# A four-layer conditioned sequence block: the next batch's opening is moved one stage ahead, into the scores and the attention tail

## The reference, cut to what matters

```python
# L0: layer norm with a conditioned bias
out = (x - mean) * rsqrt(var + 1e-5) * weight + bias + tanh(cond @ lin_w.T + lin_b)
x = out * weight + bias
# L1: bottleneck whose two matrices depend on cond (the "down" and "up" products)
down = relu(x @ Wd_b.T + bd);  x = x + down @ Wu_b.T + bu
# L2: RMS norm, up_w (2*1024 x 256), val * gelu(gate), quantised, ternary down_w, + x
# L3: adaptive RMS norm, attention with 16 heads of 16, then SwiGLU
x = x + (cond @ attn_alpha_w.T) * attention(ada_rmsnorm(x))
x = x + (cond @ ffn_alpha_w.T) * (swiglu(ada_rmsnorm(x)) @ out_w.T + out_b)
```

## Time and profile before

| what | value |
|---|---|
| median of three runs | 692.21 us |
| profiled execution | 697.42 us |
| its span on the core | 695.6 us |
| mean granted clock of TensorE | 0.972 of full speed |
| TensorE busy | 626.0 us, 90% |
| VectorE busy | 416.1 us, 60% |
| ScalarE busy | 393.5 us, 57% |
| GpSimd busy | 90.8 us, 13% |

### The profile page before, as it was taken

How to read it: one execution, slowest core, us unless ns; L and a number is a source line. 1 busy time by engine, 2 the same in 40 slices (tenths; PEclk the granted TensorE clock), 3 DMA queues, 4 the chain that set the end, 5 groups by cost and what they waited for, 6 DMA issues and landing times.

```text
span 695.6 us, 9460 instructions
## 1 busy us (share of the span) xinstructions
PE 626.0 (90%) x3495; PEld 420.0 (60%) x3495; DVE 416.1 (60%) x840; ACT 393.5 (57%) x755; POOL 90.8 (13%) x117
## 2 busy tenths in 40 slices
PE   3765798899989999999989999999899999999896
PEld 1421577754457878744458878644478787444585
DVE  0341697498536575788265765986365857881444
ACT  1322478336775558367873675467755583677610
POOL 1002330121000000631000002710000006310000
PEclk9976699999999999999999999999999999999999
DMA  8998640512000001431000005320000005210000
GB/s 261 373 356 286 191 143 31 114 24 50 1 1 1 1 1 44 101 77 25 1 1 1 0 8 110 82 47 2 2 1 0 1 7 109 68 34 2 0 1 31
DMA packets 34877, 45.06 MB, mean 65 GB/s; under 512 B 4752, under 2 KB 27920, under 8 KB 34704
## 3 DMA queue, kind: packets, MB, share of 16 engines
q1 hardware_dynamic: 30128, 31.32, 16.2%
q0 software_dynamic: 3488, 10.49, 5.4%
q10 hardware_dynamic: 1216, 2.66, 1.4%
HBM read 28.45 MB, written 3.15 MB: 45 GB/s over the span
## 4 chain that ended last, share of the span: by engine, by line
PE 61%; DVE 14%; ACT 10%; DMA 8%; issue 3%; SPq 2%; ACTq 1%
PE psum L1314 27%; PE psum L1566 8%; DVE mx L1143 8%; PE psum L1555 7%; PE psum L1512 7%; DMA arena<-in_hyp_w 3%; DMA early_pieces<-in_hyp_w 3%; PE psum L1458 2%; DMA kst<-split 2%; ACT arena L615 2%; PE psum L1394 2%; PE psum L1594 2%; PE psum L1403 1%; ACT arena L689 1%; ACT act L615 1%
## 5 line engine op out<-in xcount | busy, mean ns | idle before, releaser
L1143 DVE TENSOR_REDUCE mx<-psum 128x1 f32<-128x512 f32 x256 | 159.7, 683 | 32.0 <-PE psum L1512 32.0
L829 ACT ACTIVATE arena<-psum 128x512 f32<-128x512 f32 x256 | 140.5, 601 | 61.0 <-PE psum L1555 59.3
L1314 PE MATMUL psum<-act,ghw_hi 128*128 128x512 f32 (+1 forms) x288 | 88.5, 375 | 3.0 <-DVE act L955 2.5
L1512 PE MATMUL psum<-kst,qst 96*128 96x512 f32 x192 | 79.2, 437 | 2.9 <-DMA kst<-split 1.2
L1555 PE MATMUL psum<-qst,kst 98*128 98x512 f32 x192 | 77.6, 425 | 1.8 <-ACT arena L829 1.8
L1314 PE MATMUL psum<-upw_hi,kst 128*128 128x512 f32 x256 | 72.2, 404 | 0.0
L452 POOL DMA_DIRECT2D kst<-split x36 | 18.0, 505 | 411.7 <-DMA kst<-split 371.1
L1566 PE MATMUL psum<-arena,vals 128*17 128x512 f32 x512 | 67.4, 598 | 1.4 <-ACT arena L829 1.0
L1314 PEld LDWEIGHTS psum<-act,ghw_hi 128*128 128x128 f32 x288 | 51.9, 188 | 14.6 <-DVE act L955 4.7
L1512 PEld LDWEIGHTS psum<-kst,qst 96*128 96x128 f32 x192 | 36.1, 189 | 40.4 <-DVE mx L1143 30.4
L1314 PEld LDWEIGHTS psum<-upw_hi,kst 128*128 128x128 f32 x256 | 47.1, 191 | 9.6
(11 more groups left out here) (199 smaller groups left out, 1109.2 us busy)
## 6 DMA issues: line engine op xcount, KB each, us to landing
early_pieces<-in_hyp_w SPq DMA_DIRECT2D x17, 512.0 KB, 8.7
arena<-in_hyp_w SPq DMA_DIRECT2D x15, 512.0 KB, 8.5
qst<-split SPq DMA_DIRECT2D x72, 64.0 KB, 3.5
kst<-split POOLq DMA_DIRECT2D x36, 128.0 KB, 3.6
arena<-in_x SPq DMA_DIRECT2D x4, 512.0 KB, 3.5
arena<-in_up_w POOLq DMA_DIRECT2D x8, 256.0 KB, 4.0
arena<-in_gh_w POOLq DMA_DIRECT2D x8, 256.0 KB, 3.3
out_x<-arena SPq DMA_DIRECT2D x8, 256.0 KB, 2.1
```

Source lines behind the costliest of these rows:

```text
L829: s.activation(probs[:, kb % 2, i, :], bank[3 + n % RING], ACT.Exp).then_inc(a_p, 1)
L1143: v.reduce_max(mx[:, g % 2, col:col + 1], bank[u % RING], AX.X).then_inc(d_max, 1)
L1314: ins = pe.matmul(dst, lhs(a, c), rhs(z, c), start=start and n == 0, stop=stop and n == len(terms) - 1, skip_group_check=skip)
L1512: pe.matmul(bank[u % RING], qst[g % 3][0:KROWS, i, P * t:P * t + P], keys_of(g)[0:KROWS, i // 2, :], start=True, stop=True).then_inc(e_max, 1)
```

## The change

The next batch's front starts one stage earlier, and its last parts leave the feed-forward stage.

- Norm: GpSimd now takes the power -1/2 of the variance (`front_root`, two operations of 128x4) instead of ScalarE's root and VectorE's reciprocal, and VectorE's `front_norm` stands in score group 3, directly behind the statistics and the weights.
- Turn: in two parts of four transposes (`front_turn_part`), into banks 5 and 6, one in front of and one behind `turn_heads` of the last group.
- x1: ScalarE writes only the two high parts (`front_x1_high`), in the tail. VectorE makes the full value from PSUM itself (`front_x1`, into a new place `x1T`) and the low part (`front_x1_low`).
- Down product: behind the attention output, into bank 7; the Relu pair of `front_bottleneck` stands between `half_affine` and the first Silu, its low part on VectorE in front of block 0.
- Alphas: for batches 1 to 3 the product is made in two halves of 256 columns in the tail of the batch before (bank 6), around the transposes of the norm. VectorE makes `wo_alpha` from PSUM and copies the second half to a place that alternates between the two halves of the tile `alpha` (`ff_alpha`). In batch 0 it stays where it was.
- The up product and what follows it move one block forward; the three products of `keep_clock` in the tail go, except in the last batch.

```diff
-FRONT_BANK = (6, 7)
+FRONT_BANK, DOWN_BANK, ALPHA_BANK = (5, 6), 7, 6
...
+            def front_root(f):
...
+                pool.wait_ge(d_mv, f + 1)
+                pool.sem_inc(keys_free, 1)
+                pool.tensor_scalar(stat[:, RS0, :], mv[:, :, 1], 1e-5, None, ALU.add).then_inc(p_rs0, 1)
+                pool.wait_ge(p_rs0, 2 * f - 1)
+                pool.tensor_tensor(stat[:, RS0, :], stat[:, RS0, :], neg_half.to_broadcast([P, T]), ALU.pow
+                                   ).then_inc(p_rs0, 1)
...
                 if not last:
-                    deviation(b + 1)
+                    front_x1_high(b + 1, 0)
                 for h in range(2):
                     heads_turned(1, h)
+                if not last:
+                    front_x1_high(b + 1, 1)
...
+                if not last:
+                    front_bottleneck(b + 1)
                 for f in range(HT if last else NOW):
...
                     if not last:
-                        if f == 0:
-                            front_x1(b + 1)
                         if f == 1:
-                            front_bottleneck(b + 1)
-                        if f == 2:
                             front_h2(b + 1)
...
+            def front_x1(f, c):
+
+                v.wait_ge(a_x1, (f + 1) * C + c + 1)
+                step(v.tensor_scalar(x1T[:, c, :], bank[FRONT_BANK[c]], w_sq[:, c:c + 1],
+                                     prm_all[:, f, Q_B0 + c:Q_B0 + c + 1], ALU.mult, ALU.add))
...
+            def front_alphas(f):
+
+                v.wait_ge(e_alpha, f + 1)
+                v.wait_ge(p_wo_alpha, 1)
+                v.tensor_tensor(wo_alpha[:, :, :], vow[:, 1, :].rearrange("p (c d) -> p c d", c=C),
+                                bank[ALPHA_BANK][:, 0:D].unsqueeze(1).to_broadcast([P, C, D]), ALU.mult)
...
+                            condition(b + 1)
+                            front_norm(b + 1)
...
                 if not last:
-                    front_norm(b + 1)
+                    front_x1(b + 1, 0)
+                    front_x1_low(b + 1, 0)
+                    front_x1(b + 1, 1)
                 for h in range(2):
                     pair = slice(2 * h, 2 * h + 2)
                     v.wait_ge(e_wo, b * 2 + h + 1)
...
+                if not last:
+                    front_x1_low(b + 1, 1)
...
+                if not last:
+                    front_bottleneck(b + 1)
+                    front_alphas(b + 1)
...
-                        if g == 1 and k == AT_ALPHA:
+                        if g == 1 and k == AT_ALPHA and first:
                             alphas()
...
-                if not last:
-                    front_turn(b + 1)
-                keep_clock(bank[0], 6 if last else 3)
+                if last:
+                    keep_clock(bank[0], 6)
+                else:
+                    front_down(b + 1)
+                    front_alphas(b + 1, 0)
                 for h in range(2):
                     turn_half(b, h, d_xn4, e_n2T, bank[4 + h], xn4)
+                if not last:
+                    front_alphas(b + 1, 1)
...
                     if f == 0 and not last:
-                        pe.wait_ge(a_x1, (b + 1) * (2 * C) + 2 * C)
+                        pe.wait_ge(a_dn, (b + 2) * 2)
+                        pe.wait_ge(d_alpha, b + 2)
...
                     if not last:
                         if f == 1:
-                            front_down(b + 1)
-                        if f == 2:
                             front_up(b + 1)
```

More of the change, by code:

```diff
@@ L123, in build @@
         consts = sb("consts", [P, 4])
-        eps5, eps6, magic = consts[:, 0:1], consts[:, 1:2], consts[:, 2:3]
+        eps5, eps6, magic, neg_half = [consts[:, k:k + 1] for k in range(4)]
         bn = sb("bn", [P, T, 6])
@@ L152, in build, with ff_alpha @@
         kept_hh = (kept_even, kept_odd)
+        def ff_alpha(b):
+            return alpha[:, D:2 * D] if b % 2 == 0 else alpha[:, 0:D]
         hidden_raw = hypw[:, 1, :]
@@ L562, in batch @@
                 alphas(b, first)
+                if b < B - 1:
+                    front_root(b + 1)
             batch(0, first=True)
@@ L641, in front_x1, with front_x1_high @@
                 affine(f, e_l0T, lambda c: bank[banks[c]], slice(0, L), None, Q_B0, inp[0], a_x1, full)
+            def front_x1_high(f, c):
+                s.wait_ge(e_l0T, f * C + c + 1)
+                s.activation(inp[0][:, c, :], bank[FRONT_BANK[c]], ACT.Identity, scale=w_sq[:, c:c + 1],
+                             bias=prm_all[:, f, Q_B0 + c:Q_B0 + c + 1]).then_inc(a_x1, 1)
             def front_bottleneck(f, full=dn_f):
@@ L645, in front_bottleneck @@
                 for dst in (dn_s[0], full):
-                    s.activation(dst, bank[4], ACT.Relu, bias=vec[:, V_BD:V_BD + 1]).then_inc(a_dn, 1)
+                    s.activation(dst, bank[4 if f == 0 else DOWN_BANK], ACT.Relu, bias=vec[:, V_BD:V_BD + 1]).then_inc(a_dn, 1)
             def front_h2(f):
@@ L1050, in batch @@
             def batch(b, last, first=False):
-                v.tensor_copy(cond_bc[:, :], condT[:, bass.ds(b, 1)].to_broadcast([CND, P])).then_inc(d_prm, 1)
+                if first:
+                    condition(0)
                 v.wait_ge(d_rs2, b + 1)
@@ L1180, in batch @@
                             u += 1
-                        if g == 1 and k == ALPHA_OUT:
-                            if not first:
-                                v.wait_ge(p_kept_ff, b * 2)
+                        if g == 1 and k == ALPHA_OUT and first:
                             alphas()
@@ L1337, in front_turn, with front_turn_part, front_alphas @@
                 turn(f, d_xn, e_l0T, [bank[k] for k in banks], x_tok)
+            def front_turn_part(f, c):
+                pe.wait_ge(d_xn, f * T + T)
+                for t in range(T):
+                    ins = pe.transpose(bank[FRONT_BANK[c]][:, P * t:P * t + P], x_tok[:, t, P * c:P * c + P], ident[:, :])
+                ins.then_inc(e_l0T, 1)
+            def front_alphas(f, h):
+                if h == 0:
+                    pe.wait_ge(d_prm, f + 1)
+                    pe.wait_ge(a_x1, (f + 2) * C)
+                ins = pe.matmul(bank[ALPHA_BANK][:, D * h:D * h + D], cond_bc[:, :], alphaw[:, D * h:D * h + D],
+                                start=True, stop=True)
+                if h == 1:
+                    ins.then_inc(e_alpha, 1)
             def front_down(f, first=False):
@@ L1341, in front_down @@
                 pe.wait_ge(d_x1, f * C + C)
-                product(bank[4], lambda a, c: hyp_s[a][:, c * BN:(c + 1) * BN], lambda a, c: inp[a][:, c, :],
+                product(bank[4 if first else DOWN_BANK], lambda a, c: hyp_s[a][:, c * BN:(c + 1) * BN], lambda a, c: inp[a][:, c, :],
                         range(C)).then_inc(e_down, 1)
@@ L1651, in batch @@
                 weigh(NG - 1, T - 1)
+                if not last:
+                    front_turn_part(b + 1, 0)
                 for h in range(2):
                     turn_heads(NG - 1, h, range(2 * h, 2 * h + 2))
+                if not last:
+                    front_turn_part(b + 1, 1)
                 for h in range(2):
@@ L1693, in batch @@
                     ins.then_inc(e_gh, 1)
-                    if f == 4 and not last:
+                    if f == 3 and not last:
                         front_x2tok(b + 1)
```

52 lines of the change are left out of this document (34 added, 18 removed).

## The result

The changed kernel takes 698.19 us (median of 22 runs, 693.63 to 701.81) where the kernel before, on the same chip, takes 693.59 us (22 runs, 690.56 to 698.57). The ratio is 1.0059, 95% interval [1.0043, 1.0076]: slower by 0.6%. Forecast were 690.6 us and no change. A second measurement of both, further down, gives 1.0055 [1.0031, 1.0078].

A forecast was written before the change was run, and what follows sets the result against it. It took one TensorE stream, held in places by other engines, as the bound. Three steps of +2.0 + 0.15 - 1.4 give +2.25, with scores -3.9 makes -1.65 us: 692.21 to 690.6 us, range 686.5 to 695.5.

The forecast's parts named there:

- some tails: Rival: TensorE's clock falls in one or two tails, about 1.4 us a tail, 692.0 to 693.4 us; chance 0.14.
- Slower: Rival: clock falls in all three tails from the down product into feed-forward, 1.9 us or more each, 696.3 us; chance 0.07.
- Tail, +2.0: Tail: down product and alpha half before the turn start `half_affine` 2.0 us later, 0.7 of the addition included.
- First block, +0.15: First feed-forward block: TensorE waits 0.8 us for Relu, table and alphas, instead of 0.65 us for `front_x1`: +0.15 us.
- Down product gone from the stream, -1.4: Feed-forward stream on TensorE: `front_down` is missing from it, 1.4 us less a step.
- scores, -1.3: Scores of batches 1 to 3: without the alpha product and its copy, 1.3 us less a batch, -3.9 us over three.
- Norm in the scores, 0: Scores: norm and condition copy hide in VectorE's 6.96 us idle time if GpSimd's two operations take under about 5 us; cost 0.
- Turn and x1 fit into the tail's pauses: Tail: eight transposes fit TensorE's waits within 0.1 us; ScalarE's x1 fits its wait, but VectorE's addition comes 0.7 us later.
- if the granted clock is 0.5 anywhere behind the pause: Sign named beforehand that the prediction is wrong: half clock behind TensorE's pause of about 2 us before the down product.
- the tail is nearly free: Rival: engine pauses in the tail take up the moved work, delay 1.6 us, scores give 1.6; 686.1 us; chance 0.21.
- GpSimd's power is slow: Rival: power over 10 us makes the norm hold up VectorE's last heads; at 12 us, 696 us; chance 0.03.
- The table rule: Rival: a 1.38 us drain behind table loads; if only behind the Relus, hidden block 1.1 us later a step, 693.9; chance 0.03.

The follow-up runs named there:

- b_nokeep: The kernel before without its three clock-keeping products in the tails of batches 0 to 2; 693.63 us, ratio to before 1.0010.
- after_again: The changed kernel, unaltered, measured once more on the chip of the variants; 697.10 us, ratio to before 1.0055.
- fill8: The changed kernel with eight 128x512 products without use in TensorE's pause before the down product, batches 0 to 2; 692.89 us, ratio to before 0.9996.
- alpha_back: fill8 with the alpha product of batches 1 to 3 put back among the score tiles; 696.46 us, ratio to before 1.0026.
- pe_order: The changed kernel with nine filling products and, on TensorE, first-half turn, down product, second-half turn, then alphas; 687.76 and 689.00 us, ratios to before 0.9922 and 0.9936.
- no_fill: The changed kernel, pause unfilled, with first-half turn before the down product and VectorE's additions and first norm before x1 chunk 1; 693.02 us, ratio to before 0.9989.

## Why the prediction was wrong, point by point

**The step that failed** is the choice of full clock for the forecast, together with the sentence on the clock-keeping products, "they stood in front of a wait and cost nothing". Their removal is not the whole of it: in the kernel before, where the gap that they leave is 0.90 us, it costs nothing that can be measured (b_nokeep); here it leaves a pause of 1.98 us without cover. The prediction had seen the pause of 2 us, had found the same pause before the one fall in the trace, and then gave clock falls only 0.14 and 0.07. From the down product on, one fall makes a step of after 1.4 to 2.3 us longer than its undisturbed one. That is the mechanism of both clock rivals: *some tails* by the count (two of three tails in each of the two profiles), *Slower* by the place, the reach and the price (1.9). That *Slower* forecast 696.3 us, 4.1 us above its 692.21, and that the measured loss is 0.0059 x 693.59 = 4.1 us too, is partly luck: it took three falls off a gain of 1.65 us. The profile of after_again has two falls of 2.15 us, 4.3 us, less a gain of 0.1 to 0.3 us in each of the three steps, which makes its three steps 4.0 us longer than before's. The argument against it, "one case, not a rule, and the places around the pause are busy", was the wrong way round: one pause of that length was known, and it had fallen. The Trainium skill's "TensorE: Matmul & The Clock Gate", section "HAM oscillation", which says that kernels that wait between bursts come back at half clock, agrees with this in kind; the traces add that it does not happen behind every such pause.

**Term by term, at full clock** (step 1 of after, and fill8, whose steps average 148.07 against before's 148.34). Split at the first output product, the step is:

| | before | fill8 | difference | forecast |
|---|---|---|---|---|
| mark to first output product | 15.95 | 18.14 | +2.19 | +2.15 |
| from there to the next mark | 132.39 | 129.93 | -2.46 | -2.7 |
| step | 148.34 | 148.07 | -0.27 | -0.55 |

- *Tail, +2.0*: `half_affine` is 2.33 us later (9.35 against 7.02). Several terms were a little short: x1 of chunk 1 takes 0.81 us and not 0.69, the down product keeps the queue for 1.53 us (200.95 to 202.48) and not 1.40, the alpha half for 0.63 and not 0.55, the turn until `half_affine` 0.69 and not 0.6. With the alpha half gone altogether `half_affine` comes 0.79 us sooner (alpha_back).
- *First block, +0.15*: TensorE's wait before the output product is 0.51 us (from VectorE) instead of 0.8, less than before's 0.65, so this term is -0.14. VectorE's four operations ahead of the block take 2.67 us together (208.01 to 210.68), and not the 2.99 of their added lengths. That the sum of the two terms is right to 0.04 is luck: their errors have opposite signs.
- *Down product gone from the stream, -1.4, and scores, -1.3*: together -2.46; by alpha_back the scores are -1.22, which leaves -1.24 for the first, if nothing else changed in that stretch.
- *Norm in the scores, 0*: right. GpSimd's power takes 1.32 us and VectorE waits 0.81 us for it at 183.39, in its idle time.
- *Turn and x1 fit into the tail's pauses*: right; the attention output starts 2.50 us behind the mark in both kernels, and VectorE waited 0.17 us for ScalarE before x1 of chunk 1.

So the mechanism was right at each place it was worked out, and the sum at full clock is -0.8 us over three steps where -1.65 was forecast. Against the falls that error is small. Of the signs named beforehand, "if the granted clock is 0.5 anywhere behind the pause" came, and so did a step that grows.

**Of the other rivals**: *the tail is nearly free* did not come in this queue order, as the prediction argued, but pe_order reaches 687.8 and 689.0 us, nearer to its 686.1, with the same work in the tail. *GpSimd's power is slow* did not come either (1.32 us). The table rule: in after the load begins at 208.73 and the Silu at 210.02, 1.29 us later. That leaves no room for the drain of 1.38 us that the Trainium skill's "ScalarE: Activation LUTs", section "What ACT_TABLE_LOAD costs", puts behind the load; the measurement decides.

What stays open: why the pause of 1.98 us brings a fall in some tails and none in others of the same execution, and why the low time is once 3.4 and once 10.2 us. Whether three products, as before had, would have been cover enough was not run; four were.

## What to carry to other kernels

When a change gives an in-order engine a new pause, price two things apart: the delay at full clock, and what the work behind the pause costs at half clock if the clock falls; the second decides where that work stands on the path, and a few products without use in the pause tell at once whether it does. Put moved work behind the instruction that another engine waits for, and give it its input early, so that the in-order queue never waits in front of the critical handover: with the moved products ahead of the first transposes the first output product is 2.2 us later than before (fill8), with them behind it is 0.6 us later (pe_order). If the stretch before the region varies from execution to execution, compare marks within the region and not spans.

## What the runs showed of the hardware that I had not expected

- The low stretches behind TensorE's pauses have two lengths: 3.4 us (after's third tail, one in no_fill, the one in b_nokeep) and 10.2 us (one in after, two in after_again, one in no_fill).
- Of nine tails in three executions with an uncovered pause of 1.77 to 1.98 us, six fell. With eight or nine products in it, none of 24 did; with four, none of three. But a pause need not be that long: in b_nokeep one of three tails fell behind pauses of 0.90 and 0.43 us.
- At half clock the down product grew from 1.61 to 2.90 us (no_fill) and the eight transposes from 1.09 to 1.97 (after), 1.8 times in both.
- A power of 128x4 numbers on GpSimd takes 1.32 us and an addition of the same size 0.23 us; the 128x512 product there is 1.27 us.
- VectorE's operation with two scalar operands from PSUM, 128x512, takes 0.80 to 0.81 us, longer than the copy (0.68) and than the one with three operands (`SCALAR_TENSOR_TENSOR`, L1074, 0.75).
